# A last channel split 3:1 between VectorE and ScalarE, outputs summed by group, and zero matmuls ahead of TensorE's waits

## The chip, the cores and the metric

The kernel runs on one core of one Trainium2 chip. The metric is device time in microseconds (us). Each time shown is one run of the whole program, and several runs are summed up by their median.

## The reference, cut to what matters

```python
Q, K, V = (x @ W + b, split in H = 16 heads of D = 8)      # x: 8 batches, 512 rows, 128 columns
for wl in range(16):                                        # 16 "channels"
    scores = (Q * cpm[wl]) @ (K * cpm[wl]).T * SCALE        # cpm = cos(phase_modulators)
    scores = scores * cos(KERR * scores * scores)           # KERR = 2.7e-12
    acc += softmax(scores) @ V * interference_weights[wl]
attn = (acc / 16, heads joined) @ Wo + bo
```

Behind it stand a layer norm, a gated network for all rows, a network of 8 experts for 256 chosen rows, and a last layer norm. For these inputs the cosine is 1 within rounding, and a flag that the kernel works out on the chip takes it into a fast branch without the cosine. The scores of channel wl are then the same Q.K products times cpm[wl] squared, so per head and batch one matrix of scores serves all 16 channels: each needs exp(c2[wl] * score), a product with V, and a sum for the denominator, which is a column of ones beside V.

## The kernel before, in words

Work is cut into 32 units. A unit is one head (of 16) for one group of 4 batches (of 2 groups). Its scores, turned so that keys lie on partitions, stand in s_t as 4 key tiles (kt) of 4 batches of 512 queries: 128 partitions by 8192 f32. There are two buffers of it, `s_t[:, p]`, for even and odd units.

Each unit has 16 steps, w = 0 to 15, one per channel. In a step ScalarE makes `probs[:, w % 2] = exp(c2 * s_t[:, p])` over all 8192 columns (L597), and TensorE multiplies it with V: 16 matmuls of 128 by 27 weights and 512 columns, four at a time in the four column strips of the array (L1200). Three channels share one PSUM bank as a group, told apart by where their 9 columns stand in zero padding, so the 16 channels make six groups: steps 0-2, 3-5, 6-8, 9-11, 12-14, and 15 alone. When a group is full, VectorE copies the bank to `o_sb` (L1385), TensorE transposes that copy (`turn_products`, L1178 to L1184), and VectorE takes the reciprocal of the denominators, multiplies it with the channel weight, and multiplies the outputs with that into `weighted` (`weigh`, L1361 to L1373). At the end of the unit one reduction over the 16 channels writes the head's columns of `comb` (L1395).

In step 15 only half of the exponentials are ScalarE's: key tiles 2 and 3, 4096 columns. VectorE computes those of key tiles 0 and 1 with a polynomial, in four pieces of 1024 columns (`piece_dve`, L659 to L687), whose parts are written out by hand between its other work (`PIECE_STEPS`). TensorE multiplies the pieces with V at steps 4, 8, 11 and 15 (`piece_pe`, L690 to L700, `PRODUCT_STEPS`).

The next unit's scores are prepared during the present one, with a fixed step for each part (`prep_pe` and `prep_dve`): projection at step 1, four row maxima at steps 2 to 5, a transposition at step 6, and four tiles of scores at steps 8 to 11, each copied by VectorE into `s_t[:, 1 - p]` (L791). For the second group of batches (16 units), the layer norms and the gated network of the first group's rows are also spread over the two units of a loop turn (`FF_STEPS`, m = 16 p + w): m = 12, 13, 15, 16, 23, 27, 28 and 29. The stages at m = 13, 27 and 29 each hold a layer norm on VectorE.

What sets the order: each engine works through its own list in program order, and counters tie them together. ScalarE's step w waits until the product of step w - 2 has freed its `probs` buffer, and at w = 0 until all four tiles of the unit's `s_t` are copied. TensorE's step w waits for the exponentials of step w. The first product of a group waits until the bank has been copied out. `turn_products` waits for that copy and for the `weigh` before. Every second unit closes a turn of a loop on each engine (ScalarE L585, TensorE L1174, VectorE L1356). There are two such loops of eight turns, one per group of batches.

```python
pe.wait_ge(s["exp_done"], u * W + (w + 1))                 # TensorE, before the products of step w
act.wait_ge(s["pv_done"], u * W + (w + 1))                 # ScalarE; pv_done begins at 2
n0 = DVE_KT * NB * S if w == W - 1 else 0
nc.scalar.activation(probs[:, w % 2, n0:], s_t[:, p, n0:], ACT.Exp, scale=scales[w % 2])
```

Of the kernel before, what the change touches and what calls it, by code (L numbers as in the profile page):

```python
# [6 lines left out]
ALU = mybir.AluOpType  # L7
ACT = mybir.ActivationFunctionType
AX = mybir.AxisListType
# [38 lines left out]
BIASED_MAGIC = float(1.5 * 2 ** 23 + 127)  # L48
LOWEST_Y = -126.0
EXP2 = (1.0000000005541674, 0.6931472057372656, 0.24022646890630472, 0.05550328776967869, 0.009618488957523083,  # L50
        0.00133999312182961, 0.00015345811891707452)
# [36 lines left out]
def postln_kernel(nc, a):  # L88
    with ExitStack() as ctx:
# [12 lines left out]
        weighted = sb("weighted", [P, W, GT * D])  # L102
        x_next = weighted[:].rearrange("p w n -> p (w n)")
# [11 lines left out]
        x_p = sb("x_p", [P, X_COLS])  # L115
        x_2k = sb("x_2k", [P, X_COLS], BF16)
        c2_last = sb("c2_last", [P, H])
# [91 lines left out]
        x_sq = sb("x_sq", [P, NT + 1])  # L209
# [15 lines left out]
        cos_small = sb("cos_small", [P, 3, NB])  # L225
# [8 lines left out]
        def products_of(wg):  # L234
# [11 lines left out]
                 "qa_ready st_done st_copied exp_done pv_done o_copied ot_done rz_done norm_done comb_done prep_chain chain "  # L246
# [306 lines left out]
        def _(act):  # L553
# [105 lines left out]
        def piece_dve(dve, piece, part, u, p, h):  # L659

            n = u * PIECES + piece
            link = Linked(dve, s["piece_chain"], n * PART_LINKS[3] + PART_LINKS[part])

            a = [c * (-1) ** i for i, c in enumerate(EXP2)]

            def horner(*coefficients):
                for c in coefficients:
                    link(nc.vector.scalar_tensor_tensor(out=x_p[:], in0=x_p[:], scalar=c, in1=x_y[:], op0=ALU.add, op1=ALU.mult))  # L668
# [13 lines left out]
            if part == 1:  # L682
                horner(a[5], a[4], a[3])
# [752 lines left out]
```

## Time and profile before

| | |
|---|---|
| Median of 3 runs | 3671.42 us (3670.53 to 3673.81) |
| The profiled execution's own time | 3674.77 us |
| Its span, from the first to the last instruction | 3672.7 us |
| ScalarE (ACT) busy | 3476.3 us, 95% |
| VectorE (DVE) busy | 2934.6 us, 80% |
| TensorE (PE) busy with matmuls | 2688.7 us, 73% |
| Mean granted TensorE clock | 0.882 of full speed |

Busy time is the time in which an engine has an instruction in work; waiting, branching and issuing DMAs do not count. Matmuls overlap, and their ends are modelled. In rows of the trace, `out<-in` names what an instruction writes and reads, `xN` how many there are, and the text in brackets how long the engine was idle before it and what ended that time.

### The profile page before, as it was taken

The numbers are of one execution on the slowest core, as the hardware profiler recorded it, in microseconds if no ns is written. First come the engines' busy times: TensorE is split into PE (matmuls) and PEld (weight loads), VectorE is DVE, ScalarE is ACT, GpSimd is POOL, SyncE is SP. The second block draws the span as 40 slices with busy tenths as digits, with TensorE's granted clock in tenths as the row PEclk, the third lists the DMA queues.
The fourth block names the chain that finished last, engine by engine and source line by source line (L and its number), as shares of the span: only waits on it lengthen the run. The fifth ranks groups of instructions, "written<-read, shape, count | busy, mean of one in ns | idle before, by whom it ended". The sixth has DMA issues, their size and how long they took to land.

```text
span 3672.7 us, 50238 instructions
## 1 busy us (share of the span) xinstructions
PE 2688.7 (73%) x19639; PEld 823.7 (22%) x19639; DVE 2934.6 (80%) x3858; ACT 3476.3 (95%) x635; POOL 55.8 (2%) x206
## 2 busy tenths in 40 slices
PE   5777777777777777777777777777777777777673
PEld 2222222222222222222222222222222222222222
DVE  6788777788777788777788888788888888888787
ACT  6999999999999999999999999999999999999971
POOL 0000000000000000000000000000000000000000
PEclk7988988888889889888889898889888888988986
DMA  1000000000000000000000000000000000000000
GB/s 46 1 1 1 1 1 1 1 1 1 1 1 1 1 1 1 1 14 1 1 2 1 4 2 4 2 4 1 2 4 2 4 2 1 4 2 4 2 26 29
DMA packets 19221, 16.65 MB, mean 5 GB/s; under 512 B 4177, under 2 KB 16866, under 8 KB 18722
## 3 DMA queue, kind: packets, MB, share of 16 engines
q1 hardware_dynamic: 18130, 12.54, 1.2%
q8 instruction: 185, 3.03, 0.3%
q14 instruction: 58, 0.48, 0.0%
q10 hardware_dynamic: 720, 0.34, 0.0%
q0 software_dynamic: 128, 0.26, 0.0%
HBM read 7.76 MB, written 5.37 MB: 4 GB/s over the span
## 4 chain that ended last, share of the span: by engine, by line
ACT 53%; issue 27%; PE 9%; DVE 4%; ACTq 4%; DMA 0%; POOL 0%; DVEq 0%; POOLq 0%
ACT probs L597 53%; PE psum L1200 7%; ACTq L590 3%; DVE x_p L668 1%; PE psum L719 1%; DVE m_pad L770 0%; ACTq L594 0%; DVE x_p L686 0%; DVE probs L843 0%; PE psum L699 0%; DVE probs L1106 0%; DVE q_s L654 0%; DVE q_t L762 0%; ACT probs L614 0%; DVE k_s L654 0%
## 5 line engine op out<-in xcount | busy, mean ns | idle before, releaser
L597 ACT ACTIVATE probs<-s_t 128x8192 f32<-128x8192 f32 (+1 forms) x512 | 3440.8, 6807 | 69.2 <-PE psum L1200 67.6
L1200 PE MATMUL psum<-probs,v_pad 128*27 128x512 f32 x15872 | 2239.1, 691 | 578.7 <-ACT probs L597 523.0
L1200 PEld LDWEIGHTS psum<-probs,v_pad 128*27 128x27 f32 x15872 | 568.4, 119 | 1976.5 <-issue 1382.2
L668 DVE SCALAR_TENSOR_TENSOR x_p<-x_p,x_y 128x1024 f32<-128x1024 f32 x640 | 782.0, 1222 | 14.2
L1385 DVE COPY o_sb<-psum 128x512 f32<-128x512 f32 x192 | 132.7, 691 | 249.9 <-PE psum L1200 237.5
L791 DVE COPY s_t<-psum 128x2048 f32<-128x2048 f32 x130 | 297.0, 2284 | 11.2 <-PE psum L749 10.2
L770 DVE TENSOR_REDUCE m_pad<-psum 128x4 f32<-128x2048 f32 x132 | 301.6, 2286 | 3.9
L699 PE MATMUL psum<-x_p,v_pad 128*27 128x512 f32 x512 | 157.1, 696 | 190.1 <-DVE x_p L686 190.1
L761 DVE TENSOR_SCALAR v_t<-psum,b_head 128x512 f32<-128x512 f32 x33 | 24.8, 751 | 208.1 <-PE psum L719 208.1
L686 DVE SCALAR_TENSOR_TENSOR x_p<-x_p,x_2k 128x1024 f32<-128x1024 f32 x128 | 156.8, 1225 | 4.4
L1184 PE MATMUL psum<-ident,o_sb 128*128 128x128 f32 x768 | 122.1, 282 | 47.9 <-DVE weighted L1373 47.9
L679 DVE SCALAR_TENSOR_TENSOR x_y<-x_p,x_y 128x1024 f32<-128x1024 f32 x128 | 156.0, 1219 | 0.0
L1395 DVE TENSOR_REDUCE comb<-weighted 128x2048 f32 x32 | 121.3, 3792 | 5.2 <-DVE weighted L1373 5.2
L675 DVE TENSOR_SCALAR x_p<-x_y 128x1024 f32<-128x1024 f32 x128 | 88.9, 695 | 38.3 <-PE psum L699 30.3
L1368 DVE RECIPROCAL r_z<-psum 128x48 f32<-128x48 f32 x192 | 80.6, 420 | 40.8 <-PE psum L1184 37.2
L729 PE MATMUL psum<-k_s,q_s 24*128 24x512 f32 x528 | 67.7, 503 | 62.2 <-DVE k_s L654 40.0
L1184 PEld LDWEIGHTS psum<-ident,o_sb 128*128 128x128 f32 x768 | 82.8, 140 | 104.7 <-issue 104.0
L1373 DVE TENSOR_TENSOR weighted<-psum,r_z 128x384 f32<-128x384 f32 x192 | 98.5, 513 | 6.7
L672 DVE TENSOR_SCALAR x_y<-s_t,c_last 128x1024 f32<-128x1024 f32 x128 | 95.3, 744 | 1.6 <-issue 1.3
L719 PE MATMUL psum<-x_group,w_head 128*32 128x512 f32 x792 | 92.8, 602 | 0.0
L681 DVE TENSOR_SCALAR x_p<-x_y 128x1024 f32<-128x1024 f32 x128 | 88.9, 695 | 4.4
L677 DVE TENSOR_SCALAR x_2k<-x_p 128x1024 int16<-128x1024 int16 x128 | 88.9, 694 | 4.4
(244 smaller groups left out, 990.8 us busy)
## 6 DMA issues: line engine op xcount, KB each, us to landing
x_next_dram<-weighted SPq DMA_DIRECT2D x1, 1024.0 KB, 3.9
x_group<-x_next_dram SPq DMA_DIRECT2D x1, 1024.0 KB, 4.9
loop_memory<-in_L_attn_x_dram SPq DMA_DIRECT2D x8, 128.0 KB, 2.1
x_dram<-loop_memory SPq DMA_DIRECT2D x8, 128.0 KB, 1.8
out_dram<-loop_memory SPq DMA_DIRECT2D x8, 128.0 KB, 1.8
x_dram<-probs SPq DMA_DIRECT2D x2, 512.0 KB, 3.6
out_dram<-probs SPq DMA_DIRECT2D x2, 512.0 KB, 3.6
s_t<-in_L_ffn_ew_dram SPq DMA_DIRECT2D x3, 256.0 KB
```

Of the source, the lines that this page charges most:

```text
L597: nc.scalar.activation(probs[:, w % 2, n0:], s_t[:, p, n0:], ACT.Exp, scale=scales[w % 2]).then_inc(s["exp_done"], 1)
L668: link(nc.vector.scalar_tensor_tensor(out=x_p[:], in0=x_p[:], scalar=c, in1=x_y[:], op0=ALU.add, op1=ALU.mult))
L679: link(nc.vector.scalar_tensor_tensor(out=x_y[:], in0=x_p[:], scalar=BIASED_MAGIC, in1=x_y[:], op0=ALU.subtract, op1=ALU.subtract))
L686: nc.vector.scalar_tensor_tensor(out=x_p[:], in0=x_p[:], scalar=a[0], in1=x_2k[:], op0=ALU.add, op1=ALU.mult).then_inc(s["piece_ready"], 1)
L699: last = nc.tensor.matmul(products_of(NWG - 1)[L * b:L * b + SLOTS * A, :], v_pad[:, p, b * T + kt, VPAD:VPAD + SLOTS * A], x_p[:, i * S:( ...
L719: last = nc.tensor.matmul(prep[L * b:L * b + L, i, :], w_head[:, p, i, :], x_group[:, b * S:(b + 1) * S], start=True, stop=True)
L770: nc.vector.tensor_reduce(m_pad[:, qt, :].rearrange("p (b l) -> p b l", l=L)[:, :, R_S:R_S + 1], banks(qt), AX.X, ALU.max, negate=True).th ...
L791: nc.vector.tensor_copy(s_t[:, p, kt * NB * S:(kt + 1) * NB * S], banks(kt).rearrange("p b q -> p (b q)")) \
L1184: last = nc.tensor.transpose(psum[:, 6, qt * P:(qt + 1) * P], o_sb[:, wg % 2, qt * P:(qt + 1) * P], ident[:])
L1200: last = nc.tensor.matmul(products_of(wg)[L * b:L * b + SLOTS * A, :], v_pad[:, p, b * T + kt, c0:c0 + SLOTS * A], probs[:, w % 2, at:at + ...
L1385: nc.vector.tensor_copy(o_sb[:, wg % 2, :], products_of(wg)).then_inc(s["o_copied"], 1)
L1395: nc.vector.tensor_reduce(comb[:, bass.ds(g * GT, GT), bass.ds((u - g * H) * D, D)].rearrange("p (b t) e -> p t b e", b=NB), weighted[:].r ...
```

## The change

It has four parts.

1. **Step 15.** `DVE_KT` goes from 2 to 3: of the last channel VectorE computes three key tiles (6144 columns) in three pieces of 2048 columns, and ScalarE the fourth (2048 columns). ScalarE writes them into a buffer of their own, `probs_last`, with no wait, and with a bias `ln_k` read from a column. For steps 0 to 14 the buffer is now `probs[:, (p + w) % 2]`, so steps 0 and 1 of a unit wait for the products of steps 13 and 14 of the one before, and step 2 for step 0's. The polynomial has degree 5 instead of 6 and is scaled so that its top coefficient is 1 (the bias does the same to ScalarE's share), and it rounds by a conversion to int16. A piece is now two `tensor_scalar` (one f32 to int16, one int16 to int16) and six `scalar_tensor_tensor`.
2. **Sums.** `weigh` writes group 0 into `summed` and the others into a small `weighted`, which is added to `summed` at once. At the unit's end two additions of 128 columns take the place of the reduction over 2048.
3. **Zero matmuls.** In every step but 2 and 7 TensorE issues 2 x 4 matmuls of the shape of the products, with zero weights (18 columns), into the bank in use, between the bank's wait and the wait for the exponentials (`spin_pe`). Pieces are multiplied at steps 6, 12 and 15.
4. **Memory.** Some small tensors share space, and the DMA scratch is 4096 bytes.

```diff
-DVE_KT = 2
-X_BATCHES = 2
-X_COLS = X_BATCHES * S
-PIECES = DVE_KT * NB // X_BATCHES
+DVE_KT = 3
+X_COLS = NB * S
+PIECES = DVE_KT
...
-PART_LINKS = (0, 4, 7, 9)
-
-PIECE_STEPS = {0: (0, 0), 2: (0, 1), 3: (0, 2), 4: (1, 0), 5: (1, 1), 7: (1, 2), 8: (2, 0), 9: (2, 1), 10: (2, 2),
-               11: (3, 0), 12: (3, 1), 13: (3, 2)}
-PRODUCT_STEPS = {4: 0, 8: 1, 11: 2, 15: 3}
+PART_LINKS = (0, 2, 3, 4, 5, 6)
+
+PIECE_STEPS = {0: (0, 0, 2), 2: (0, 2, 3), 3: (0, 3, 4), 4: (0, 4, 5),
+               5: (1, 0, 1), 7: (1, 1, 3), 8: (1, 3, 4), 10: (1, 4, 5),
+               11: (2, 0, 1), 12: (2, 1, 3), 13: (2, 3, 5)}
+PRODUCT_STEPS = {6: 0, 12: 1, 15: 2}
+SPINS = 2
+SPIN_STEPS = tuple(w for w in range(W) if w not in (2, 7))
...
-                                act.wait_ge(s["pv_done"], u * W + (w + 1))
-
-                                n0 = DVE_KT * NB * S if w == W - 1 else 0
-                                nc.scalar.activation(probs[:, w % 2, n0:], s_t[:, p, n0:], ACT.Exp,
+                                if w == W - 1:
+                                    nc.scalar.activation(probs_last[:], s_t[:, p, DVE_KT * NB * S:], ACT.Exp, bias=ln_k[:, 0:1],
+                                                         scale=scales[w % 2]).then_inc(s["exp_done"], 1)
+                                    continue
+                                act.wait_ge(s["pv_done"], u * W + (w + 2 if w > 1 else w + 1))
+                                nc.scalar.activation(probs[:, (p + w) % 2, :], s_t[:, p, :], ACT.Exp,
                                                      scale=scales[w % 2]).then_inc(s["exp_done"], 1)
...
             if part == 0:
+                dve.wait_ge(s["piece_ready"], n + 1)
+                link(nc.vector.tensor_scalar(x_n, scores, scale, LOWEST_Y, ALU.mult, ALU.max))
+                link(nc.vector.scalar_tensor_tensor(out=x_y[:], in0=scores, scalar=scale, in1=x_n, op0=ALU.mult, op1=ALU.subtract))
+            if part == 1:
+                nc.vector.tensor_scalar(x_n, x_n, 127.0, 128.0, ALU.add, ALU.mult)
 
                 dve.wait_ge(s["piece_used"], n + 1)
+                link(nc.vector.scalar_tensor_tensor(out=x_p[:], in0=x_y[:], scalar=K_EXP2[4], in1=x_y[:], op0=ALU.add, op1=ALU.mult))
+            if part == 2:
+                horner(K_EXP2[3])
+            if part == 3:
+                horner(K_EXP2[2])
+            if part == 4:
+                horner(K_EXP2[1])
+                nc.vector.scalar_tensor_tensor(out=x_p[:], in0=x_p[:], scalar=K_EXP2[0], in1=x_2k[:],
                                                op0=ALU.add, op1=ALU.mult).then_inc(s["piece_ready"], 1)
...
+        def spin_pe(w, wg, p):
+
+            for r in range(SPINS if w in SPIN_STEPS else 0):
+                for b in range(NB):
+                    nc.tensor.matmul(products_of(wg)[L * b:L * b + VPAD, :], v_pad[:, p, b * T, 0:VPAD],
+                                     s_t[:, p, b * S:(b + 1) * S], start=(w in FIRST_OF and w < W - 1), stop=(w in FIRST_OF and w < W - 1))
...
-                                pe.wait_ge(s["exp_done"], u * W + (w + 1))
                                 if w in FIRST_OF:
 
                                     wg = FIRST_OF[w]
                                     pe.wait_ge(s["o_copied"], u * NWG + (wg + 1))
+                                spin_pe(w, wg, p)
+                                pe.wait_ge(s["exp_done"], u * W + (w + 1))
...
+                                dst = (weighted if wg else summed)[:, 0:n, :]
+                                dve.wait_ge(s["sum_done"], u * NWG + max(wg, 1))
...
+                                if wg:
+                                    dve.wait_ge(s["norm_done"], n1 + 1)
+                                    nc.vector.tensor_tensor(summed[:, 0:n, :], summed[:, 0:n, :], dst, ALU.add) \
+                                        .then_inc(s["sum_done"], 1)
...
-                            nc.vector.tensor_reduce(
+                            nc.vector.tensor_tensor(weighted[:, 0, :], summed[:, 0, :], summed[:, 1, :], ALU.add) \
+                                .then_inc(s["sum_done"], 1)
+                            dve.wait_ge(s["sum_done"], u * NWG + (NWG + 1))
+                            nc.vector.tensor_tensor(
                                 comb[:, bass.ds(g * GT, GT), bass.ds((u - g * H) * D, D)].rearrange("p (b t) e -> p t b e", b=NB),
```

## Rows read from the trace of the kernel before

**Rows 1.** The page, parts 1 and 2: busy time of each engine, and TensorE's clock in 40 slices

```profile
PE 2688.7 (73%) x19639; PEld 823.7 (22%) x19639; DVE 2934.6 (80%) x3858; ACT 3476.3 (95%) x635; POOL 55.8 (2%) x206
PEclk7988988888889889888889898889888888988986
```

**Rows 2.** The longest waits: who waited for whom, us in total, times, longest

```profile
PE psum L1200 <- ACT probs L597: 523.0, 296, 3.3
ACT probs L597 <- PE psum L1200: 67.6, 43, 2.1
PE psum L1200 <- issue: 46.3, 14, 3.6
```

**Rows 3.** Groups by line and form: busy us in all, mean ns of one

```profile
L597 ACT ACTIVATE probs<-s_t 128x8192 f32<-128x8192 f32 x480 | 3328.7, 7021 | 69.2 <-PE psum L1200 67.6 <-DVE s_t L791 1.6
L597 ACT ACTIVATE probs<-s_t 128x4096 f32<-128x4096 f32 x32 | 115.3, 3602 | 0.0
```

**Rows 4.** Timeline of ScalarE around one unit: start, us, what, [idle before]

```profile
818.46 107.45 ACT L597 ACTIVATE probs<-s_t 128x8192 f32<-128x8192 f32 x16 [1.78 <-PE psum L1200]
```

**Rows 5.** Timeline of TensorE in the same unit

```profile
813.24 5.57 PE L1200 MATMUL psum<-probs,v_pad 128*27 128x512 f32 x34 [3.29 <-ACT probs L597]
...
832.48 3.64 PE L1200 MATMUL psum<-probs,v_pad 128*27 128x512 f32 x32 [1.52 <-ACT probs L597]
835.93 2.76 PE L719 MATMUL psum<-x_group,w_head 128*32 128x512 f32 x24
...
867.09 5.33 PE L1200 MATMUL psum<-probs,v_pad 128*27 128x512 f32 x32 [2.29 <-ACT probs L597]
```

**Rows 6.** TensorE at a loop's edge, units 7 to 8: its timeline

```profile
932.28 0.63 PE L1184 MATMUL psum<-ident,o_sb 128*128 128x128 f32 x4 [1.50 <-DVE weighted L1373]
936.38 5.01 PE L1200 MATMUL psum<-probs,v_pad 128*27 128x512 f32 x32 [3.47 <-issue]
```

**Rows 7.** Windows: us, TensorE busy (instructions), granted clock, DMA share, GB/s

```profile
936.00:939.00 3.00, 2.62 (x16) 0.50 0.03 5
941.50:944.50 3.00, 2.79 (x28) 1.00 0.00 0
```

**Rows 8.** VectorE at the same edge: its copy of the last group

```profile
930.24 0.69 DVE L1385 COPY o_sb<-psum 128x512 f32<-128x512 f32 x1 [1.86 <-PE psum L1200]
```

**Rows 9.** Groups by line and form of VectorE: busy us in all, mean ns of one

```profile
L668 DVE SCALAR_TENSOR_TENSOR x_p<-x_p,x_y 128x1024 f32<-128x1024 f32 x640 | 782.0, 1222 | 14.2
L679 DVE SCALAR_TENSOR_TENSOR x_y<-x_p,x_y 128x1024 f32<-128x1024 f32 x128 | 156.0, 1219 | 0.0
L1395 DVE TENSOR_REDUCE comb<-weighted 128x2048 f32 x32 | 121.3, 3792 | 5.2 <-DVE weighted L1373 5.2
L672 DVE TENSOR_SCALAR x_y<-s_t,c_last 128x1024 f32<-128x1024 f32 x128 | 95.3, 744 | 1.6 <-issue 1.3
L1373 DVE TENSOR_TENSOR weighted<-psum,r_z 128x384 f32<-128x384 f32 x160 | 89.2, 558 | 5.6
L675 DVE TENSOR_SCALAR x_p<-x_y 128x1024 f32<-128x1024 f32 x128 | 88.9, 695 | 38.3 <-PE psum L699 30.3 <-DVE x_y L672 0.2
L677 DVE TENSOR_SCALAR x_2k<-x_p 128x1024 int16<-128x1024 int16 x128 | 88.9, 694 | 4.4
```

**Rows 10.** All engines over the two loops of units: us, busy of PE, PEld, DVE, ACT, POOL, clock

```profile
55.40:3567.30 3511.90, 2629.18 (x19335) 779.17 (x19335) 2818.72 (x3569) 3437.45 (x520) 40.17 (x184) 0.89 0.01 3
```

**Rows 11.** VectorE and then TensorE ahead of a loop's edge in the second loop

```profile
2234.90 0.46 DVE L1368 RECIPROCAL r_z<-psum 128x48 f32<-128x48 f32 x1
...
2236.31 2.48 DVE L668 SCALAR_TENSOR_TENSOR x_p<-x_p,x_y 128x1024 f32<-128x1024 f32 x2
...
2239.96 0.42 DVE L921 TENSOR_TENSOR loop_memory<-psum,loop_memory 128x256 f32<-128x256 f32 x1
...
2244.49 0.68 DVE L1385 COPY o_sb<-psum 128x512 f32<-128x512 f32 x1
...
2239.07 5.75 PE L1200 MATMUL psum<-probs,v_pad 128*27 128x512 f32 x34 [1.91 <-ACT probs L597]
```

More of the change, by code:

```diff
@@ L661, in piece_dve @@
             n = u * PIECES + piece
[L662 to L668, printed above, removed]
-            if part == 0:
-                scores = s_t[:, p, piece * X_COLS:(piece + 1) * X_COLS]
-                link(nc.vector.tensor_scalar(x_y[:], scores, c2_last[:, bass.ds(h, 1)], LOWEST_Y, ALU.mult, ALU.max))
-                dve.wait_ge(s["piece_used"], n + 1)
-                link(nc.vector.tensor_scalar(x_p[:], x_y[:], BIASED_MAGIC, None, ALU.add))
-                low_halves = x_p[:].bitcast(I16).rearrange("p (n o) -> p n o", o=2)[:, :, 0:1]
-                nc.vector.tensor_scalar(x_2k[:].bitcast(I16).rearrange("p (n o) -> p n o", o=1), low_halves, 7, None,
-                                        ALU.logical_shift_left)
-                link(nc.vector.scalar_tensor_tensor(out=x_y[:], in0=x_p[:], scalar=BIASED_MAGIC, in1=x_y[:],
-                                                    op0=ALU.subtract, op1=ALU.subtract))
-                link(nc.vector.tensor_scalar(x_p[:], x_y[:], a[6], None, ALU.mult))
@@ L682, in piece_dve, with horner @@
-            if part == 1:
-                horner(a[5], a[4], a[3])
-            if part == 2:
-                horner(a[2], a[1])
-                nc.vector.scalar_tensor_tensor(out=x_p[:], in0=x_p[:], scalar=a[0], in1=x_2k[:],
+            link = Linked(dve, s["piece_chain"], n * PART_LINKS[5] + PART_LINKS[part])
+            scores = s_t[:, p, piece * X_COLS:(piece + 1) * X_COLS]
+            scale = c2_last[:, bass.ds(h, 1)]
+            def horner(c):
+                link(nc.vector.scalar_tensor_tensor(out=x_p[:], in0=x_p[:], scalar=c, in1=x_y[:], op0=ALU.add, op1=ALU.mult))
@@ L690, in piece_pe @@
         def piece_pe(pe, piece, u, p):
-            pe.wait_ge(s["piece_ready"], u * PIECES + (piece + 1))
+            pe.wait_ge(s["piece_ready"], u * PIECES + (piece + 2))
             if piece == 0:
                 pe.wait_ge(s["o_copied"], u * NWG + 2)
-            kt, b0 = piece * X_BATCHES // NB, piece * X_BATCHES % NB
-            for i in range(X_BATCHES):
-                b = b0 + i
-                last = nc.tensor.matmul(products_of(NWG - 1)[L * b:L * b + SLOTS * A, :], v_pad[:, p, b * T + kt, VPAD:VPAD + SLOTS * A],
-                                        x_p[:, i * S:(i + 1) * S], start=(kt == 0), stop=False)
-            last.then_inc(s["piece_used"], 1)
+            for b in range(NB):
+                last = nc.tensor.matmul(products_of(NWG - 1)[L * b:L * b + SLOTS * A, :], v_pad[:, p, b * T + piece, VPAD:VPAD + SLOTS * A],
+                                        x_p[:, b * S:(b + 1) * S], start=(piece == 0), stop=False)
+            last.then_inc(s["piece_used"], 1)
+        def spin_pe(w, wg, p):
+            for r in range(SPINS if w in SPIN_STEPS else 0):
+                for b in range(NB):
+                    nc.tensor.matmul(products_of(wg)[L * b:L * b + VPAD, :], v_pad[:, p, b * T, 0:VPAD],
+                                     s_t[:, p, b * S:(b + 1) * S], start=(w in FIRST_OF and w < W - 1), stop=(w in FIRST_OF and w < W - 1))
         def prep_pe(pe, step, n, p, group, first=False):
@@ L1201, in _ @@
                                             products_of(wg)[L * b:L * b + SLOTS * A, :], v_pad[:, p, b * T + kt, c0:c0 + SLOTS * A],
-                                            probs[:, w % 2, at:at + S], start=(kt == 0 and w in FIRST_OF),
+                                            probs[:, (p + w) % 2, at:at + S] if w < W - 1 else probs_last[:, b * S:(b + 1) * S],
+                                            start=(kt == 0 and w in FIRST_OF),
                                             stop=(kt == T - 1 and w in LAST_OF))
```

41 lines of the change are left out of this document (26 added, 15 removed).

## The prediction

> **What bounds the kernel now.** I read the page first: ScalarE is busy for 95% of the span, VectorE for 80%, TensorE for 73%, and TensorE's clock is nowhere steadily at full speed [rows 1]. The waits come next: ScalarE waits for TensorE's products, 67.6 us in 43 waits; TensorE waits far longer for ScalarE; and TensorE has 14 gaps of 3.3 us each (46.3 / 14) in which it waits for nothing that the profile shows [rows 2]. The groups give ScalarE's two prices, 7.02 us for 8192 columns and 3.60 us for 4096 [rows 3]. Its timeline shows that sixteen of them run back to back in 107.45 us, so that one takes 6.92 us from start to start ((107.45 - 3.60) / 15), and that the idle time of 1.78 us stands once per unit, at the unit's border [rows 4]. So ScalarE sets the time: what shortens its work or its waits counts in full, and all else only as far as it makes ScalarE wait.
>
> TensorE's two speeds matter below. Sixteen products take 3.64 us in one step and 5.33 us in another [rows 5], and the windows show what differs: the granted clock is 0.50 (1.2 GHz) just after a long gap and 1.00 (2.4 GHz) later [rows 7]. At full speed the next work starts 3.45 us after the first product, so four matmuls cost 0.86 us, at 1.2 GHz 1.73 us. In the two loops of units the mean clock is 0.89 [rows 10].
>
> **The change part by part.**
>
> *ScalarE's last part.* From 8192 to 4096 columns saves 3.42 us, so 2048 columns fewer save half of that, 1.71 us, and leave 1.89 us. All of it is on the bounding engine: 32 x 1.71 = **54.7 us less**. The bias read from a column is new. I take it at nothing, since no row shows one. The Trainium skill ("ScalarE: Activation LUTs", section "What ACT_TABLE_LOAD costs") gives about 93 ns for such an operand, which would add 3 us.
>
> *The own buffer.* ScalarE waits at each border because step 0 needs the buffer of step 14, whose products take 5.57 us, part of them at 1.2 GHz, while step 15 gives only 3.60 us of cover [rows 5]. Afterwards step 0 needs step 13's and step 1 needs step 14's, one exponential later. The cover rises from 3.6 to 1.9 + 6.9 = 8.8 us. So **up to 67.6 us less** [rows 2]. In the second loop other work crowds in and some waits will stay: I leave a tenth, 7 us.
>
> *VectorE.* Per unit the pieces go from 4 x (0.744 + 3 x 0.695 + 1.22 + 5 x 1.222 + 1.225) = 45.5 us to 3 x (two `tensor_scalar` and six `scalar_tensor_tensor` of 2048 columns). From 384 and 1024 columns with two tensors (558 and 1219 ns) one column costs 1.03 ns and the start 0.16 us, so 2048 columns cost 2.28 us; the one-tensor form (695 ns for 1024) comes to 1.23 us, 1.28 with a scale [rows 9]. That makes 3 x 16.2 = 48.6 us. Bounds for the two int16 forms, which no row shows at this shape: 1.23 us, or 2.28 us if they run no faster than the two-tensor form, which would make 54.9 us. I take 1.23, since the int16 row nearest to them costs 694 ns for 1024 columns, like f32. The Trainium skill ("VectorE: DVE Perf Modes", section "What auto-detection actually checks") says that a one-source operation with 16-bit input and output in SBUF runs twice as fast again; that would be about 0.69 us for one of the two and take 52 us off VectorE in all, but nothing off this sum. The sums trade 3.79 us for 4 x 0.56 + 3 x 0.29 = 3.1 us. VectorE goes from 88.1 us per unit (2818.72 / 32) [rows 10] to 90.5 of about 106: no bound on average, and I cost it at nothing except where it is late, below.
>
> *Zero matmuls.* 14 steps x 2 x 0.86 = 24 us per unit on TensorE. It is busy 82.2 us per unit now (2629.18 / 32) at clock 0.89 [rows 10], about 73 us at full speed, so 97 of 106 us. They fill its waits for the exponentials, and the 5.33 us steps should become 3.64 us. Their cost is nothing where ScalarE's result comes later anyway. But they stand ahead of the products in TensorE's list: **where TensorE is late already, they make it later.**
>
> *The loops' edges.* That place is the end of each loop turn, after every second unit, 14 times in all, where TensorE stands still for 3.3 us between turns [rows 2, 6]. Let T be the end of step 14's exponentials. Step 14's products, the piece, the zero matmuls and step 15's products take 3.45 + 0.86 + 1.73 + 0.86 + 0.19 = 7.1 us. VectorE copies, and the last transposes start 2.04 us after its copy did [rows 6, 8], so at T + 9.2, end at T + 9.8, and the gap lasts to T + 13.1. The clock is at 1.2 GHz after that gap [rows 7], so the zero matmuls of step 0 take 3.45 us and its products 3.64 to 5.01 us: done between T + 20.2 and T + 21.6. ScalarE has meanwhile done 15, 0 and 1, by T + 1.9 + 2 x 6.9 = T + 15.7, and its step 2 waits for the products of step 0. It loses 4.5 to 5.9 us, I take 5.1. Before the change the 1.8 us at the border was all it lost there. Seven edges in the first loop: **36 us more**.
>
> In the second loop VectorE has a layer norm in m = 27 and another in m = 29. Now the queue ahead of its copy of group 4 is two 1.22 us steps, the last one, then the norm from 2239.96 to 2244.49, so that the copy starts 5.4 us after the products of step 14 did, with no idle time before it [rows 11]. Afterwards those three steps take 6.9 us instead of 3.7, and the three before `weigh` some 5.8 instead of 3.7: up to 5.3 us later. The copy then comes at T + 10 to 10.8 and the last transposes at T + 12 to 13.4 (instead of T + 9.2), and ScalarE loses 7.3 to 10.1 us at the edge. I take 8.5: seven edges make **60 us more**. At the last unit the 1.7 us of step 15 lies beside this queue and the queue delays the tail: 4 us more.
>
> *The rest* (memory, setup, tail) moves nothing that waits.
>
> **Sum:** -54.7 - 67.6 + 7 + 36 + 60 + 4 = -15.3 us, which takes the span from 3672.7 to 3657.4 us. The profiled execution took 3674.77 us itself, 2.1 us of it around the span, and stands 3.35 us above the median of 3671.42. I put the difference on the median: **3656 us**. About 0.2% (7.3 us) is what a measurement of this kernel can tell from no change.
>
> **The rivals.**
>
> *The edges cost more (slower).* Place: the step after each edge, above all in the second loop. If the int16 forms cost 2.28 us and nothing absorbs VectorE's queue, the stalls are about 8 and 11 us: 7 x 19 = 133 us, 37 more than above, 3693 us. It decides from a mean stall of 8.0 us instead of 6.8. For it: VectorE's copy has no slack there [rows 11]. Against it: VectorE idles elsewhere, and ScalarE's own stall gives it time.
>
> *Zero weights do not hold the clock up (the change doesn't do what it says).* Then TensorE needs 97 / 0.89 = 109 us per unit, over ScalarE's 106, and becomes the bound: 3 us x 32, about 3750 us. It decides below a granted clock of about 0.92. Nothing in the trace speaks for or against zero operands; the zero padding beside V already passes through the array.
>
> *The edges cost half.* If the clock has recovered by the time of step 0, the zero matmuls take 1.73 and the products 3.64 us: the first loop's stall falls to 2.8 us, and if VectorE's queue is absorbed, the second's to 4: 47 us less, 3608 us.
>
> *The edges cost nothing* (the gap hidden): 3656 - 96 = 3560 us. Against it: the gap is 3.47 us on TensorE itself, with nothing behind it that could run [rows 6].
>
> **How the numbers follow.** The forecast has 0.50, with its own range 3640 to 3675; of that 0.36 is faster by over 0.2% (below 3664), 0.12 within it, 0.02 slower. Heavier edges: 0.20 (0.17 slower, 0.03 same). Clock not held: 0.06, slower. Edges at half: 0.16, and at nothing: 0.08, faster. Together faster 0.60, same 0.15, slower 0.25. The range of 3600 to 3698 us takes in the forecast, the heavier edges and the half case, and leaves out the clock, the hidden gap and the outer parts of the others, some 0.18.
>
> **What would show it.** Right: ScalarE's last form at about 1.9 us; hardly any wait of ScalarE at the units' borders inside a turn, but 14 waits of 4 to 10 us for products, two exponentials behind each edge, longer in the second loop; TensorE's busy time up by some 450 us (774 for the zero matmuls, less 9 x 32 for the better clock), with a clock near 0.97; sixteen products mostly at 3.64 us. Wrong: ScalarE's waits well under 70 us (half or no edges) or over 130 us (heavier), a clock under 0.92, or `tensor_scalar` rows of 2.3 us.

## The result, and the profile after

| | before | after |
|---|---|---|
| Median | 3675.55 us (6 runs, 3670.53 to 3688.33) | 3654.65 us (6 runs, 3653.28 to 3655.35) |
| Profiled execution, its span | 3674.77, 3672.7 us | 3655.35, 3653.1 us |
| Mean granted clock | 0.882 | 0.962 |

The ratio, of the means of the runs, is 0.9937, with a 95% interval of 0.9918 to 0.9955: faster by 0.6%. The forecast was 3656 us. One run of the kernel with turns of four units (3712.93 us, granted clock 0.833) was in a slower state of the chip and is left out of the numbers below. ScalarE does 54 us less work but waits 29 us more, so more than half of the gain was given back.

The page, parts 1 and 2, against [rows 1]:

```profile
PE 3118.8 (85%) x26807; PEld 916.9 (25%) x26807; DVE 2978.9 (82%) x3412; ACT 3422.7 (94%) x635; POOL 66.8 (2%) x206
PEclk7999999999999999999999999999999999999996
```

TensorE works 430 us more, nearly all at full clock, and ScalarE 53.6 us less. The longest waits, against [rows 2]:

```profile
PE psum L1213 <- ACT probs L606: 232.0, 225, 1.8
ACT probs L606 <- PE psum L1213: 97.0, 15, 9.5
PE psum L713 <- issue: 43.8, 14, 3.6
DVE x_2k L680 <- issue: 24.0, 8, 3.4
PE psum L704 <- DVE x_p L693: 5.8, 8, 0.9
```

ScalarE now waits 15 times instead of 43, but 97.0 us instead of 67.6. The 14 gaps of TensorE that nothing releases are all still there; they end at the first zero matmul of a turn (L713). The groups by form, against [rows 3, 9]:

```profile
L606 ACT ACTIVATE probs<-s_t 128x8192 f32<-128x8192 f32 x480 | 3330.1, 7026 | 98.6 <-PE psum L1213 97.0 <-DVE s_t L803 1.6
L602 ACT ACTIVATE probs_last<-s_t,ln_k 128x2048 f32<-128x2048 f32 x32 | 63.8, 1995 | 0.0
L680 DVE TENSOR_SCALAR x_2k<-s_t,c_last 128x2048 int16<-128x2048 f32 x96 | 123.0, 1281 | 32.9 <-issue 24.0 <-DVE comb L1422 8.9
L683 DVE TENSOR_SCALAR x_2k<-x_2k 128x2048 int16<-128x2048 int16 x96 | 66.1, 689 | 1.1
```

ScalarE's last part costs 1.995 us. VectorE's new forms lie where the prediction had them, but for the one from int16 to int16 (L683), which takes 0.689 us. Over both loops, against [rows 10]:

```profile
55.60:3547.70 3492.10, 3059.18 (x26501) 872.51 (x26502) 2864.96 (x3119) 3383.84 (x520) 51.14 (x184) 0.98 0.01 3
```

Per unit that is 95.6 us for TensorE (3059.18 / 32), 89.5 for VectorE (2864.96 / 32) and 105.7 for ScalarE. TensorE bounds no unit on average. The place that matters is a loop's edge. TensorE's timeline at one edge of the first loop, against [rows 6]:

```profile
912.80 3.64 PE L1213 MATMUL psum<-probs,v_pad 128*27 128x512 f32 x32 [1.58 <-ACT probs L606]
916.25 1.04 PE L704 MATMUL psum<-x_p,v_pad 128*27 128x512 f32 x8
917.11 1.90 PE L713 MATMUL psum<-s_t,v_pad 128*18 128x512 f32 x16
918.83 1.04 PE L1213 MATMUL psum<-probs_last,v_pad 128*27 128x512 f32 x8
...
921.97 0.63 PE L1196 MATMUL psum<-ident,o_sb 128*128 128x128 f32 x4 [1.52 <-DVE weighted L1391]
925.99 3.60 PE L713 MATMUL psum<-s_t,v_pad 128*18 128x512 f32 x16 [3.39 <-issue]
929.37 3.65 PE L1213 MATMUL psum<-probs,v_pad 128*27 128x512 f32 x32
```

and ScalarE's beside it:

```profile
912.65 1.98 ACT L602 ACTIVATE probs_last<-s_t,ln_k 128x2048 f32<-128x2048 f32 x1
914.54 13.94 ACT L606 ACTIVATE probs<-s_t 128x8192 f32<-128x8192 f32 x2
933.09 7.03 ACT L606 ACTIVATE probs<-s_t 128x8192 f32<-128x8192 f32 x1 [4.62 <-PE psum L1213]
```

Take T = 912.7, the end of step 14's exponentials. TensorE's last transposes start at T + 9.3, its gap ends at T + 13.3, the zero matmuls behind it take 3.4 us at the low clock, and the products of step 0 end at T + 20.3, while ScalarE has been ready for step 2 since T + 15.8. It crosses the unit's border with no wait and stands still 4.62 us two exponentials later. The clock by windows, against [rows 7]:

```profile
926.00:930.00 4.00, 4.00 (x24) 0.57 0.02 4
930.00:934.00 4.00, 4.00 (x43) 1.00 0.00 0
```

TensorE at an edge of the second loop, against [rows 11]:

```profile
2212.63 3.62 PE L1213 MATMUL psum<-probs,v_pad 128*27 128x512 f32 x32
2217.11 1.06 PE L704 MATMUL psum<-x_p,v_pad 128*27 128x512 f32 x8 [0.86 <-DVE x_p L693]
...
2224.42 0.63 PE L1196 MATMUL psum<-ident,o_sb 128*128 128x128 f32 x4 [1.48 <-DVE weighted L1391]
2228.12 3.62 PE L713 MATMUL psum<-s_t,v_pad 128*18 128x512 f32 x16 [3.07 <-issue]
2231.51 4.51 PE L1213 MATMUL psum<-probs,v_pad 128*27 128x512 f32 x32
```

VectorE at the same edge:

```profile
2210.12 4.61 DVE L676 SCALAR_TENSOR_TENSOR x_p<-x_p,x_y 128x2048 f32<-128x2048 f32 x2
2214.76 2.29 DVE L693 SCALAR_TENSOR_TENSOR x_p<-x_p,x_2k 128x2048 f32<-128x2048 f32 x1
2216.97 0.42 DVE L933 TENSOR_TENSOR loop_memory<-psum,loop_memory 128x256 f32<-128x256 f32 x1
...
2221.55 1.28 DVE L1409 COPY o_sb<-psum 128x512 f32<-128x512 f32 x2
```

And ScalarE behind it:

```profile
2236.10 20.88 ACT L606 ACTIVATE probs<-s_t 128x8192 f32<-128x8192 f32 x3 [8.89 <-PE psum L1213]
```

VectorE works without a pause from 2181 to 2222 us. Its pieces and its layer norm put the copy (L1409) 8.9 us behind the start of step 14's products, where it was 5.4 us before [rows 11], and ScalarE's wait is twice that of the first loop.

### The profile page after: what moved, and what is told of

It is laid out like the page before. It is cut to its first block, busy times and chain, and to the rows that moved or that the text cites. A ratio compares the mean times of both kernels' runs of the same rounds, so it can differ in the third digit from the quotient of the medians.

```text
span 3653.1 us, 63568 instructions
## 1 busy us (share of the span) xinstructions
PE 3118.8 (85%) x26807; PEld 916.9 (25%) x26807; DVE 2978.9 (82%) x3412; ACT 3422.7 (94%) x635; POOL 66.8 (2%) x206
## 4 chain that ended last, share of the span: by engine, by line
ACT 46%; issue 33%; DVE 9%; PE 7%; ACTq 4%; DMA 0%; POOL 0%; DVEq 0%; POOLq 0%
ACT probs L606 45%; ACTq L597 3%; PE psum L1213 3%; DVE x_p L676 2%; PE psum L713 2%; ACT probs_last L602 1%; DVE s_t L803 1%; DVE x_y L681 1%; DVE weighted L1391 0%; DVE x_p L686 0%; PE psum L1196 0%; DVE r_z L1384 0%; ACTq L605 0%; DVE o_sb L1409 0%; DVE x_2k L680 0%
## 5 line engine op out<-in xcount | busy, mean ns | idle before, releaser
L606 ACT ACTIVATE probs<-s_t 128x8192 f32<-128x8192 f32 x480 | 3330.1, 7026 | 98.6 <-PE psum L1213 97.0
L1213 PE MATMUL psum<-probs,v_pad 128*27 128x512 f32 x15360 | 1760.4, 599 | 237.2 <-ACT probs L606 232.0
L713 PE MATMUL psum<-s_t,v_pad 128*18 128x512 f32 x7168 | 906.8, 626 | 48.0 <-issue 43.8
L1213 PEld LDWEIGHTS psum<-probs,v_pad 128*27 128x27 f32 x15360 | 460.7, 107 | 1506.5 <-issue 1023.0
L676 DVE SCALAR_TENSOR_TENSOR x_p<-x_p,x_y 128x2048 f32<-128x2048 f32 x288 | 658.9, 2288 | 5.5
L713 PEld LDWEIGHTS psum<-s_t,v_pad 128*18 128x18 f32 x7168 | 187.2, 100 | 507.2 <-issue 499.6
L1409 DVE COPY o_sb<-psum 128x512 f32<-128x512 f32 x192 | 131.9, 690 | 119.9 <-PE psum L1213 105.4
L681 DVE SCALAR_TENSOR_TENSOR x_y<-s_t,c_last,x_2k 128x2048 f32<-128x2048 f32 x96 | 225.8, 2352 | 3.4
L693 DVE SCALAR_TENSOR_TENSOR x_p<-x_p,x_2k 128x2048 f32<-128x2048 f32 x96 | 220.0, 2292 | 3.3
L686 DVE SCALAR_TENSOR_TENSOR x_p<-x_y 128x2048 f32<-128x2048 f32 x96 | 219.5, 2287 | 0.0
L773 DVE TENSOR_SCALAR v_t<-psum,b_head 128x512 f32<-128x512 f32 x33 | 24.8, 751 | 196.9 <-PE psum L731 196.9
L680 DVE TENSOR_SCALAR x_2k<-s_t,c_last 128x2048 int16<-128x2048 f32 x96 | 123.0, 1281 | 32.9 <-issue 24.0
L704 PE MATMUL psum<-x_p,v_pad 128*27 128x512 f32 x768 | 101.4, 600 | 5.8 <-DVE x_p L693 5.8
```

What stands on the lines that cost most here:

```text
L606: nc.scalar.activation(probs[:, (p + w) % 2, :], s_t[:, p, :], ACT.Exp, scale=scales[w % 2]).then_inc(s["exp_done"], 1)
L680: link(nc.vector.tensor_scalar(x_n, scores, scale, LOWEST_Y, ALU.mult, ALU.max))
L681: link(nc.vector.scalar_tensor_tensor(out=x_y[:], in0=scores, scalar=scale, in1=x_n, op0=ALU.mult, op1=ALU.subtract))
L686: link(nc.vector.scalar_tensor_tensor(out=x_p[:], in0=x_y[:], scalar=K_EXP2[4], in1=x_y[:], op0=ALU.add, op1=ALU.mult))
L713: nc.tensor.matmul(products_of(wg)[L * b:L * b + VPAD, :], v_pad[:, p, b * T, 0:VPAD], s_t[:, p, b * S:(b + 1) * S], start=(w in FIRST_OF ...
L1213: last = nc.tensor.matmul(products_of(wg)[L * b:L * b + SLOTS * A, :], v_pad[:, p, b * T + kt, c0:c0 + SLOTS * A], probs[:, (p + w) % 2, a ...
```

## The experiments

Twelve kernels were run. The kernel before, timed with each of them, had medians of 3669 to 3677 us; so experiments are compared by their ratios to it, 0.001 of which is 3.7 us. A ratio has an interval of about 0.002 either way, so the difference of two of them is uncertain by some 10 us. ScalarE's waits for products (97.0 us in the changed kernel) are a second measure, from one profiled execution each. Waits and spans are of the profiled executions.

### TensorE's turns written out

```diff
-                    with pe.Fori(g * H // 2, (g + 1) * H // 2) as i:
+                    for i in range(g * H // 2, (g + 1) * H // 2):
```

> The changed kernel with TensorE's two loops of units written out, so that its list has no loop edge between units; the other engines keep their loops. If the loop edges are what eats the gain (14 gaps, then zero matmuls at 1.2 GHz), the seven stalls of ScalarE in the first loop (34 us together) vanish whole, turns of the first loop take 2 x 105.9 = 212 us, and the second loop keeps some 3 to 5 us per turn from VectorE's queue: about 70 us less than the changed kernel, near 3585 us. If TensorE is simply too full with the zero matmuls, ScalarE keeps most of its 97 us of waits, in other places, and the time stays above 3640 us. If VectorE's queue alone makes the second loop's stalls, they stay at 8 to 9 us each and only the first loop's 34 us go: about 3620 us.

Measured: 3586.13 us, ratio 0.9774 (0.9754 to 0.9794), span 3576.7 us (the profiled execution took 3578.85 us, 7 us less than the median). That is 0.0163, or 60 us, better than the changed kernel; by the waits it is 72 us. The gaps of TensorE "<- issue" between turns are gone. ScalarE's waits for products and its timeline at one edge of each loop:

```profile
ACT probs L606 <- PE psum L1213: 24.8, 8, 4.5
```

```profile
899.58 48.55 ACT L606 ACTIVATE probs<-s_t 128x8192 f32<-128x8192 f32 x7
...
2190.92 27.82 ACT L606 ACTIVATE probs<-s_t 128x8192 f32<-128x8192 f32 x4 [3.17 <-PE psum L1213]
```

In the first loop ScalarE runs through the edge without a wait. In the second 3.2 us a turn are left, with no gap on TensorE. So the edges are the cause of the lost gain, but not of all of it. What is left is not shown by this run; VectorE's queue is the candidate, and a run below tries it.

### Turns of four units

```diff
-                    with pe.Fori(g * H // 2, (g + 1) * H // 2) as i:
-                        for p in range(2):
+                    with pe.Fori(g * H // 4, (g + 1) * H // 4) as i4:
+                        for i, p in [(i4 * 2 + j, p) for j in range(2) for p in range(2)]:
```

> The changed kernel with TensorE's loops in turns of four units instead of two: 6 loop edges instead of 14. If a price per edge holds, 8 of 14 edges' stalls go, all but what VectorE's queue leaves: about 40 us less than the changed kernel, near 3615 us. If the gap at an edge grows with the length of a turn (twice the instructions), the gain is smaller; if the edges don't matter, the time stays at 3655 us.

Measured: 3619.04 us (median of three runs), ratio 0.9863 (0.9837 to 0.9888), span 3619.6 us.

```profile
ACT probs L606 <- PE psum L1213: 65.0, 11, 10.2
PE psum L713 <- issue: 22.9, 6, 5.0
```

Six gaps instead of 14, 27 us better (32 us by the waits): a bit under half of what writing all out brings, and less than the 40 us expected. One gap is a little longer now (22.9 / 6 = 3.8 us instead of 3.1). In the first loop ScalarE waits 4.4 to 5.9 us at the three edges that are left and nowhere between them, so there the cost goes with the number of edges. In the second loop it waits 9.1 to 10.2 us at the edges and still 3.2 to 6.1 us where an edge was taken away.

### Zero matmuls left out at step 0, and everywhere

```diff
-SPIN_STEPS = tuple(w for w in range(W) if w not in (2, 7))
+SPIN_STEPS = tuple(w for w in range(W) if w not in (0, 2, 7))
```

> The changed kernel without the zero matmuls of step 0 alone. If they stand at 1.2 GHz ahead of the products of step 0 behind each edge, the 14 stalls get shorter by up to 3.4 us each, some of it given back by products that then run more at 1.2 GHz: about 25 to 30 us less, near 3628 us, and the stalls of the first loop at 1.5 to 4 us instead of 4 to 5.8. If the gap itself and the slow products are the whole price, the time stays within 10 us of 3655 us.

Measured: 3632.53 us, ratio 0.9900 (0.9882 to 0.9918), span 3627.2 us; ScalarE waits 75.2 us. TensorE behind an edge:

```profile
918.68 6.03 PE L1213 MATMUL psum<-probs,v_pad 128*27 128x512 f32 x32 [3.16 <-issue]
```

The 3.4 us of zero matmuls are gone, but the products in their place take 6.03 us instead of 3.65. The work directly behind the gap runs at the low clock, be it useful or not, so only 1.0 us of the 3.4 is saved between the end of the gap and the end of the products here. Over the 14 edges ScalarE's waits fall by 1.5 us each. The gain is 14 us by the ratios and 22 us by the waits, less than the 25 to 30 us expected.

```diff
-SPINS = 2
+SPINS = 0
```

> The changed kernel with no zero matmuls at all. If their good (the clock at full speed) is worth less than their harm at the edges, this is faster: about 20 us less, near 3635 us, with the granted clock back at 0.87 to 0.90 and waits of ScalarE now also inside the units. If they are needed to keep TensorE ahead of ScalarE, this is slower than 3655 us by 20 us or more.

Measured: 3619.16 us, ratio 0.9864 (0.9846 to 0.9881), span 3615.4 us, clock 0.882.

```profile
ACT probs L606 <- PE psum L1213: 60.5, 15, 6.8
```

The clock falls back to that of the kernel before, and the kernel is 27 us faster than with zero matmuls by the ratios, and 36.5 us by the waits (60.5 us instead of 97.0). It came out lower than the 3635 us or so that I had put on it. So the zero matmuls do what they were built for (clock 0.882 to 0.962), and here it costs.

> The changed kernel with TensorE's loops written out and no zero matmuls. If the zero matmuls do harm at the edges alone and no good elsewhere, this equals the one with both loops written out and zero matmuls, 3586 us, within 7 us, with the clock back near 0.88. If they do good away from the edges, it is slower than 3586 us by 10 us or more; if they also do harm in the second loop, faster.

This is the edit of the first experiment and that of the fourth together. Measured: 3582.18 us, ratio 0.9753 (0.9732 to 0.9774), span 3580.3 us, clock 0.903. It and the written-out kernel with zero matmuls (0.9774) have overlapping intervals; ScalarE waits 26.7 us in the one and 24.8 in the other. So the zero matmuls' harm is at the edges alone, and nowhere does the higher clock win anything that can be measured; the intervals leave room for some 10 us either way.

### The own buffer taken back

ScalarE's last part goes into the shared buffers again, which alternate by `w % 2` as before:

```diff
-                                    nc.scalar.activation(probs_last[:], s_t[:, p, DVE_KT * NB * S:], ACT.Exp, bias=ln_k[:, 0:1],
+                                    act.wait_ge(s["pv_done"], u * W + (w + 1))
+                                    nc.scalar.activation(probs[:, w % 2, DVE_KT * NB * S:], s_t[:, p, DVE_KT * NB * S:], ACT.Exp, bias=ln_k[:, 0:1],
...
-                                act.wait_ge(s["pv_done"], u * W + (w + 2 if w > 1 else w + 1))
-                                nc.scalar.activation(probs[:, (p + w) % 2, :], s_t[:, p, :], ACT.Exp,
+                                act.wait_ge(s["pv_done"], u * W + (w + 1))
+                                nc.scalar.activation(probs[:, w % 2, :], s_t[:, p, :], ACT.Exp,
```

> The changed kernel with ScalarE's last part back in the shared probs buffers and the waits of the kernel before (step w waits for the products of step w - 2, also at step 15). If the own buffer is what took the border's waits away, they return at all 32 borders (about 1.5 to 2 us each, 50 to 67 us in all); at the 14 edges they lie inside the longer stall, so that the time rises by some 25 to 35 us, to about 3685 us. If the steady clock had already taken those waits away, the time stays within 7 us of 3655 us.

Measured: 3684.01 us (10 runs), ratio 1.0025 (1.0011 to 1.0039), span 3681.0 us: a little slower than the kernel before, and 32 us slower than the changed one. The waits, and ScalarE's timeline at an edge and at the border behind it:

```profile
ACT probs L607 <- PE psum L1214: 123.3, 46, 4.6
```

```profile
923.70 13.96 ACT L607 ACTIVATE probs<-s_t 128x8192 f32<-128x8192 f32 x2 [1.87 <-PE psum L1214]
940.62 90.12 ACT L607 ACTIVATE probs<-s_t 128x8192 f32<-128x8192 f32 x13 [2.97 <-PE psum L1214]
...
1034.50 20.88 ACT L607 ACTIVATE probs<-s_t 128x8192 f32<-128x8192 f32 x3 [1.87 <-PE psum L1214]
```

The border's wait is back at every unit, but the one behind the edge has fallen from 4.62 to 2.97 us: ScalarE, delayed at the border, needs less of TensorE later. At this edge the two waits together are 4.84 us, where the one with the own buffer was 4.62: the buffer removes a wait and all of it comes back two steps on. Only at the borders inside a turn is it a pure gain.

> TensorE's loops written out, with ScalarE's last part in the shared buffers and the old waits. With no edge to hide behind, the border's wait of 1.87 us stands at all 32 borders: 60 us over the 3586 us of the written-out loops, less what lies beside the second loop's stall of 3.2 us, so 3635 to 3645 us. If the own buffer were worth only what it was worth with the edges in place (29 us), 3615 us.

The same edit with TensorE's turns written out. Measured: 3636.23 us, ratio 0.9905 (0.9881 to 0.9928), span 3634.8 us; ScalarE waits 80.3 us in 38 waits, 55.5 us more than with the own buffer. Without the edges the buffer is worth 0.0131, or 48 us, and with them 0.0088, or 32 us.

### A part of the layer norm moved by one step

```diff
-FF_STEPS = {12: 1, 13: 2, 15: 3, 16: 4, 23: 5, 27: 5.5, 28: 6, 29: 7}
+FF_STEPS = {12: 1, 13: 2, 15: 3, 16: 4, 22: 5, 23: 5.5, 28: 6, 29: 7}
```

> The changed kernel with TensorE's loops written out and two stages of the second loop moved: the one at m = 23 to 22 and the layer norm at m = 27 to 23, where VectorE idles for 4 us at step 8, away from the copy of group 4. If VectorE's queue ahead of that copy makes the remaining stall of 3.2 us per turn, it vanishes: the second loop's turns go from 215.0 to 212 us, 25 us less than with the loops written out alone, near 3562 us. If that stall has another cause, the time stays at 3586 us.

With the turns written out, measured: 3565.31 us, ratio 0.9704 (0.9682 to 0.9725), span 3565.1 us; ScalarE's waits for products are 14.3 us in 9, where they were 24.8. In the second loop they fall from 3.2 us a turn to between 0.4 and 2.1 us, so they shrink and do not vanish. Most of the 3.2 us was thus VectorE's queue in front of the copy, from which the layer norm of m = 27 is gone. The run moved two stages at once and doesn't tell them apart.

> The changed kernel, loop edges and zero matmuls kept, with the stage at m = 23 moved to 22 and the layer norm at m = 27 to 23. If the second loop's stalls are longer than the first's by VectorE's queue alone (8.6 against 4.9 us), they fall to about 5 to 5.5 us: some 23 us less, near 3632 us. If the loop edge alone makes them, the time stays at 3655 us.

With the loops kept, measured: 3636.08 us, ratio 0.9906 (0.9884 to 0.9929), span 3637.9 us; 85.0 us of waits in 21. It takes 0.0031, about 11 us, off the changed kernel's time, with intervals that overlap: less than the 26 us with the turns written out. The stalls behind the second loop's edges fall nearly as expected, from 8.6 to 5.9 us on average (18.6 us in all), but six new waits in the last steps of its turns take 6.9 us back.

> TensorE's loops written out, the layer norm moved, and no zero matmuls. If they are worth nothing once edge and queue are gone, the time is that of the same kernel with them, 3565 us, within 7 us, though the granted clock falls to about 0.90. If the clock matters in the second loop, where TensorE is fullest, it is 10 us or more slower.

All three edits: 3562.85 us, ratio 0.9703 (0.9680 to 0.9726), span 3561.4 us, clock 0.899; 10.2 us of waits in 10. This is the fastest kernel of the study, by a hair and not measurably ahead of the one with zero matmuls. It is 3.0% faster than the kernel before, where the change itself gives 0.6%.

### The kernel before with TensorE's turns written out

The same edit as the first, on the kernel before.

> The kernel before, with TensorE's two loops of units written out and nothing else. If a loop edge costs only where something is queued behind it (zero matmuls) or where ScalarE's cover is gone, the edges cost this kernel nothing, and the time stays within 7 us of the kernel before. If each gap of 3.3 us costs ScalarE by itself, 14 of them make it 25 to 45 us faster.

Measured: 3711.84 us, ratio 1.0106 (1.0084 to 1.0127), span 3708.9 us. It went the other way: 39 us slower, and the reason is none that I had named. Its waits, ScalarE's timeline at a step 6, TensorE's at the step 4 before it, and the windows there:

```profile
ACT probs L597 <- PE psum L1200: 103.1, 63, 3.1
```

```profile
980.45 41.65 ACT L597 ACTIVATE probs<-s_t 128x8192 f32<-128x8192 f32 x6 [2.34 <-PE psum L1200]
```

```profile
974.20 0.62 PE L699 MATMUL psum<-x_p,v_pad 128*27 128x512 f32 x2 [2.55 <-DVE x_p L686]
...
974.67 5.70 PE L1200 MATMUL psum<-probs,v_pad 128*27 128x512 f32 x30
```

```profile
970.50:974.50 4.00, 1.40 (x12) 0.78 (x16) 3.93 (x4) 4.00 (x2) 0.00 (x0) 1.00 0.00 0
974.50:980.50 6.00, 6.00 (x40) 1.52 (x32) 5.77 (x8) 3.66 (x2) 0.00 (x0) 0.72 0.00 0
```

ScalarE's exponentials show a turn of 221.9 us here in nearly every turn, 218.5 in the kernel before (whose own second loop begins with three turns of 221.1 to 221.9 and then returns). At step 4 TensorE waits 2.55 us for VectorE's piece (L699), the granted clock falls to 0.72, the products of the step take 5.70 us, and ScalarE's step 6 waits 2.34 us for them.

The wait at step 4 is not where it begins: turns of 218.5 us have one too, of 1.74 us, and the products behind it take 3.92 us. The difference stands at step 1. In the kernel before, the gap makes step 0's products late, and step 1's follow 0.32 us behind them, at full clock:

```profile
941.72 3.64 PE L1200 MATMUL psum<-probs,v_pad 128*27 128x512 f32 x32 [0.32 <-ACT probs L597]
```

Written out, step 0's products run as soon as their exponentials are there, TensorE then idles, and step 1's take 5.33 us, at a granted clock of 0.69:

```profile
950.48 5.33 PE L1200 MATMUL psum<-probs,v_pad 128*27 128x512 f32 x32 [3.29 <-ACT probs L597]
```

The next unit's projection stands behind them, VectorE's work on it behind that, and the piece behind both. From the piece of step 15 to that of step 4 it is 38.0 us here and 36.3 us in the kernel before. The kernel before's own slow turn at 2132 us has the same rows (2.58 us idle, 5.33 us for step 1's products, 38.0 us). In the other unit of a turn of 221.9 us the piece comes at 36.3 us and ScalarE waits only 0.64 us at step 6.

The same order of work thus has two patterns that repeat themselves. The gap at the edge, which I had taken for harmless before the change, keeps step 1's products at full clock in every second unit. That it is the gap which holds that kernel in the better pattern is argued from the traces, not shown: three of its own turns are slow with the gap in place.

### The kernel before, written out, with zero matmuls

The `spin_pe` of the change, ahead of TensorE's waits for the exponentials, put on the kernel of the last experiment.

> The kernel before with TensorE's loops written out and the changed kernel's zero matmuls. That kernel without them took 3712 us, 35 us more than before, with extra waits of ScalarE at steps 5 and 6 (2.4 and 0.6 us per turn) beside the borders' 1.8 to 1.95. If products at 1.2 GHz make the extra waits and the borders' longer ones, a steady clock takes them away: turns of 216 to 218 us instead of 221.9, near 3620 to 3650 us. If the zero matmuls' own 1.7 us ahead of the products cost as much as the clock gives back, turns stay at 219 to 221 us, 3690 to 3710 us.

Measured: 3739.88 us, ratio 1.0185 (1.0149 to 1.0221), span 3735.8 us. Both theories missed: one had 3620 to 3650 us, the other 3690 to 3710. The waits, and TensorE's timeline at a step 4:

```profile
ACT probs L599 <- PE psum L1210: 128.8, 87, 4.0
```

```profile
977.43 1.06 PE L701 MATMUL psum<-x_p,v_pad 128*27 128x512 f32 x2 [2.56 <-DVE x_p L688]
...
978.30 3.11 PE L710 MATMUL psum<-s_t,v_pad 128*18 128x512 f32 x12
...
981.27 4.00 PE L1210 MATMUL psum<-probs,v_pad 128*27 128x512 f32 x30
```

ScalarE's waits at the borders fall to 0.25 us in the first loop, so there the better clock does help. But behind step 4's wait for VectorE the zero matmuls run at the low clock and stand ahead of the products, as they do behind an edge: waits of 2.3 us in even and 3.5 us in odd units of the first loop. The changed kernel has no such place: it multiplies its pieces at steps 6, 12 and 15, and TensorE waits for them 5.8 us in all (the row of L704 above). In the kernel before these waits were:

```profile
PE psum L699 <- DVE x_p L686: 190.1, 95, 3.6
```

That the product steps moved away from the pieces is a part of the change which the prediction did not price, and no run tried it alone.

## Why the prediction was right

The mechanism came out as it was told: ScalarE sets the time, its borders lose their wait, and behind each of 14 edges it stands still two exponentials later. That the time itself hit by 1.4 us is in part luck. The forecast was put on a median of 3671.42 us and meant 15 us less, a ratio of 0.9958, which lies just outside the measured interval of 0.9918 to 0.9955. With three more runs the median of the kernel before rose to 3675.55 us, and the gain is 21 us by the medians.

**ScalarE's last part.** Taken: 1.71 us less in each of 32. Measured: 3.602 - 1.995 = 1.607 us, 51.4 us in all. The difference of 0.1 us is put down to the bias: the same form with a bias takes 1.997 us in the shared buffer too, so it isn't the buffer. The prediction took it at nothing; the Trainium skill ("ScalarE: Activation LUTs", section "What ACT_TABLE_LOAD costs") gives about 93 ns for a pointer operand, and the trace agrees: 1.995 us against the 1.89 us worked out from the forms without a bias.

**The own buffer.** Taken: 67.6 us less, 7 us of it remaining. The borders of the changed kernel show no wait at all, so the 7 us did not come as waits there. But the term is not independent of the next one: the pair of runs with and without the buffer gives 32 us with the edges in place and 48 us without them.

**The edges.** Taken: 5.1 us in the first loop and 8.5 in the second, 36 + 60 = 96 us. ScalarE's waits at step 2 behind the edges are 4.1 to 5.8 us, 34.3 in all, and 7.6 to 9.5 us, 59.9 in all, and 2.8 in the first unit: together the 97.0 us of the row above. The steps of that sum stand as well: transposes at T + 9.3 (taken 9.2), end of the gap at T + 13.3 (13.1), zero matmuls of 3.4 us (3.45), products done at T + 20.3 (20.2 to 21.6); in the second loop, with T = 2211.4, VectorE's copy at T + 10.2 (10 to 10.8) and the last transposes at T + 13.0 (12 to 13.4).

What the prediction had wrong is how this splits by cause. It put all 96 us on the edge, so that the rival without edges came to 3560 us. Written out, the kernel took 3586 us: 24.8 us of waits stay, nearly all in the second loop, where VectorE's queue is late whether TensorE branches or not. Moving two stages of that queue took another 26 us (21 by the medians, 10.5 by the waits), and the time was 3565 us.

**Zero matmuls.** That TensorE would hold its clock and stay under ScalarE was right (busy 95.6 us a unit, predicted 97; clock 0.98 in the loops). They were priced only inside the edge, by the 3.45 us at step 0 and the 1.73 us of step 15. The run without any shows 27 us (36.5 by the waits), the run without those of step 0 shows 14 (22 by the waits), so those of other steps cost about as much again; which steps is not shown. The sum had them in it, but the prediction never said what it would be without them, and so did not show that this part of the change only costs. Its figure for TensorE's extra work was also added up wrongly: 774 less 9 x 32 is 486 us, not 450. Measured were 430 us.

**VectorE.** Taken 90.5 us a unit, measured 89.5. The one term that failed is the form from int16 to int16, taken at 1.23 us from the nearest row; it takes 0.689 us. The Trainium skill ("VectorE: DVE Perf Modes", section "What auto-detection actually checks") has such a form run twice as fast again, an estimated 0.69 us, and the trace agrees for L683, whose input and output are 16-bit; L680, which reads f32, takes 1.281 us. Nearly all of the gain lies in VectorE's idle time. But in the second loop one L683 stands in the stretch without a pause ahead of the edge's copy (at 2202.87 us in the edge above), so there it brings the copy forward, by an estimated 0.5 us in each of seven edges (1.23 less 0.69).

**The sum.** From the start of ScalarE's first exponential to the end of its last the loops took 3509.2 us before (51.3 to 3560.5) and 3485.0 after (51.5 to 3536.5): 24.2 us less. The terms give 51.4 - (97.0 - 67.6) = 22.0 us. The span fell by 19.6 us, so what lies outside gave back 4.6 us; the prediction had 4 for the tail. The span came out 4.3 us below the 3657.4 us forecast: 6 us for waits that did not come (103 predicted, 97.0 measured), 3.3 us the other way for the last part, and the rest not traced.

**The rivals.** Heavier edges (from a mean stall of 8.0 us): the mean is 6.7 us (94.2 / 14). Clock not held: it needed less than about 0.92, and the clock is 0.962. Edges at half: the first loop's stall was to be 2.8 us and is 4.1 to 5.8, since the zero matmuls behind the gap take 3.4 us and not 1.73. Edges at nothing: the 14 gaps and the stalls behind them are in the trace.

**What stays open.** The own buffer alone on the kernel before was not tried; nor were the summed outputs or the new product steps alone. And which condition puts the kernel before into its slower pattern of 221.9 us a turn is not known; what the traces show is the pattern and its chain, from step 1's products at the low clock to the late piece at step 4. The runs of the kernel before spread over 18 us here (3670.53 to 3688.33) and those of the changed kernel over 2. A varying number of slow turns, 3.4 us each, would do that; no trace shows it.

## What to carry to other kernels

Price filler work by where it stands in the engine's list: ahead of a wait that ends late it costs nothing, behind a stall it runs at the low clock and delays everything. Look for the gaps of an engine that are released by nothing ("<- issue") at a loop's edge, and try the turns written out before adding cleverness around them. Then measure: in the changed kernel the next queue (here VectorE's) was late at the same place, and the kernel before got slower by the same edit. And where one edit takes a wait away just ahead of another wait, the two don't add: ask what the later one would be without the first.

## What the hardware did that was not expected

TensorE's loop costs it 3.1 to 3.8 us between two turns: 43.8 / 14 in the changed kernel, 22.9 / 6 with turns of four units, nothing when written out. VectorE has such a gap too (L680 in the waits above): seven of 3.1 to 3.4 us at the second loop's edges, and one of 1.4 us at the first loop's start. With TensorE's turns written out VectorE's gap is still there, and the step 0 products that ScalarE waits for start before it ends. What VectorE's gap costs by itself no run shows, since none wrote its turns out. The Trainium skill ("Runtime: NRT & Kernel Launch", section "Instruction fetch mechanics") says that a taken branch to a page of instructions that is not at hand stalls the engine until it is fetched; the trace agrees in that the stalls go away with the branches, and no run here shows the fetch itself.

The other surprise is the kernel before: written out, with the gap taken away and nothing added, it became 1.1% slower, because ScalarE, TensorE and VectorE fell into a repeating order in which TensorE idles 3.29 us ahead of step 1 and 2.55 us at step 4, its granted clock drops to 0.69 and 0.72, and the products of these steps take 5.33 and 5.70 us. Removing a stall that ScalarE does not wait for can still move the kernel from one such pattern to another, by more (39 us) than most of the changes measured here.
